# First attention's context normalisation: split between two VectorE passes instead of one ScalarE pass

## The reference, cut to what matters

```
x = x + jnp.tanh(g_xattn[0]) * _L0_xattn_ref(_layernorm(x), ctx_1024, ctx_1024, mask, Wq, bq, Wk, bk, Wv, bv, ln_gamma, ln_beta)
...
scores = jnp.where(mask == 0, -jnp.inf, scores)
probs = jax.nn.softmax(scores, axis=-1)
context = jnp.einsum('bij,bjk->bik', probs, V)
mu = jnp.mean(context, axis=-1, keepdims=True)
var = jnp.var(context, axis=-1, keepdims=True)
normed = (context - mu) * jax.lax.rsqrt(var + EPS)
return normed * ln_gamma + ln_beta
```

## Time and profile before

| | before |
|---|---|
| runs | 553.64, 554.6, 555.0 us; median 554.6 |
| the profiled execution | 555.17 us, its span 553.2 us |
| TensorE's granted clock, mean | 0.933 |
| busy in the span: TensorE, VectorE, ScalarE, GpSimd | 500.8, 394.0, 340.7, 361.3 us |
| the first attention | the start to about 110 us |

### The profile page before, as it was taken

The page is one execution under the profiler, slowest core; times in us unless marked ns, Lnnn a source line. Parts: engine busy times, 40 slices in busy tenths (PEclk is TensorE's granted clock), DMA queues, the critical chain, the costliest instruction groups (busy, mean ns, idle before and its releaser), DMA issues.

```text
span 553.2 us, 12766 instructions
## 1 busy us (share of the span) xinstructions
PE 500.8 (91%) x3611; PEld 332.6 (60%) x3611; DVE 394.0 (71%) x1174; ACT 340.7 (62%) x997; POOL 361.3 (65%) x780
## 2 busy tenths in 40 slices
PE   6888797599999998799999999999999999999952
PEld 5767685456666665565656565666666565656520
DVE  3769788457433443358999898989999999988631
ACT  3667686412255553298777777777777777777510
POOL 3664788877045555324878787878878787877442
PEclk9979897579999999889999999999999999999965
DMA  8855340021122221000000000000000000000000
GB/s 232 154 94 150 92 145 16 24 87 54 29 73 72 81 71 52 27 5 7 15 18 14 21 11 21 11 20 12 21 11 21 11 22 11 19 12 7 11 10 5
DMA packets 32452, 24.48 MB, mean 44 GB/s; under 512 B 7912, under 2 KB 29808, under 8 KB 32352
## 3 DMA queue, kind: packets, MB, share of 16 engines
q1 hardware_dynamic: 29392, 18.17, 13.3%
q0 software_dynamic: 2272, 4.67, 2.6%
q10 hardware_dynamic: 720, 0.82, 0.6%
HBM read 16.88 MB, written 8.39 MB: 46 GB/s over the span
## 4 chain that ended last, share of the span: by engine, by line
PE 70%; POOL 5%; DVE 3%; DMA 3%; issue 3%; ACT 1%; POOLq 0%; SPq 0%; DVEq 0%
PE bank L1309 13%; PE bank L1257 12%; PE bank L1270 8%; PE bank L1248 7%; PE bank L992 5%; PE bank L1008 2%; PE bank L1281 2%; PE bank L1318 2%; PE bank L946 2%; PE bank L947 2%; PE bank L957 2%; DMA xs<-sorted_x 2%; PE bank L1244 2%; PE bank L1297 1%; PE bank L1234 1%
## 5 line engine op out<-in xcount | busy, mean ns | idle before, releaser
L1358 ACT ACTIVATE PRT<-bank 77x512 f32<-77x512 f32 x128 | 74.7, 584 | 18.2 <-PE bank L1257 18.2
L1257 PE MATMUL bank<-cst,wgu 128*77 128x128 f32 x512 | 81.0, 281 | 0.6 <-ACT wgu L1350 0.6
L1309 PE MATMUL bank<-w,xn3T 128*128 128x512 f32 x128 | 74.9, 668 | 2.5 <-DVE XN L1505 2.0
L936 POOL DMA_INDIRECT routed<-ys,to x39 | 37.3, 956 | 46.4 <-DVE ys L1139 37.0
L1350 ACT ACTIVATE wgu<-wgu,low 128x77 f32<-128x77 f32 x256 | 67.3, 346 | 0.4 <-DVE low L1451 0.3
L1257 PEld LDWEIGHTS bank<-cst,wgu 128*77 128x77 f32 x512 | 58.4, 148 | 14.9 <-issue 7.9
L1437 DVE TENSOR_TENSOR wgu<-bank,biasQ 128x616 f32<-128x616 f32 x64 | 50.9, 796 | 9.0 <-PE bank L1248 6.1
L1270 PE MATMUL bank<-PRT,VP 77*32 77x128 f32 x1024 | 54.5, 285 | 0.7 <-ACT PRT L1358 0.7
L1505 DVE TENSOR_TENSOR XN<-bank,OH 128x512 f32<-128x512 f32 x64 | 44.3, 692 | 14.1 <-PE bank L1309 11.3
L1248 PE MATMUL bank<-KB,QT 32*128 32x308 f32 x256 | 51.3, 437 | 0.0
L1444 DVE TENSOR_REDUCE top<-wgu 128x8 f32<-128x616 f32 x64 | 50.5, 789 | 1.1
(11 more groups left out here) (230 smaller groups left out, 1262.3 us busy)
## 6 DMA issues: line engine op xcount, KB each, us to landing
xs<-sorted_x SPq DMA_DIRECT2D x39, 64.5 KB, 1.8
wgu<-in_wgu SPq DMA_DIRECT2D x4, 512.0 KB
y<-routed SPq DMA_DIRECT2D x32, 64.0 KB, 1.8
out<-res SPq DMA_DIRECT2D x32, 64.0 KB, 1.7
ctxT<-in_ctxT SPq DMA_DIRECT2D x16, 77.0 KB, 2.8
mask<-in_mask SPq DMA_DIRECT2D x16, 77.0 KB, 3.5
wdn<-in_wdn SPq DMA_DIRECT2D x2, 512.0 KB
X<-in_x SPq DMA_DIRECT2D x1, 768.0 KB, 5.6
```

Source lines behind the costliest of these rows:

```text
L1257: last = nc.tensor.transpose(bP[c % 2][0:SK, j * 128:j * 128 + 128], SC[u][:, c * HG + j, :], ident)
L1309: nc.tensor.matmul(bF[:, :], xn3T[u][:, :], w2[:, k * HT:(k + 1) * HT, :], start=True, stop=True).then_inc(s["f"], 1)
L1358: nc.scalar.activation(PT[c % 2][:, :], bP[c % 2][0:SK, :], ACT.Copy if c * HG < HH else ACT.Exp).then_inc(s["pTs"], 1)
```

## The change

The normalised context was made by ScalarE as context x inverse deviation + shift, and VectorE multiplied it by gamma and added it to X. Now VectorE makes (context - mean) x gamma from PSUM in one operation per batch (`centred`), and adds that times the inverse deviation to X in one operation per batch (`residual`). ScalarE's `normed` is gone, and so are GpSimd's two operations for the shift. `shifted` moved behind `attend_stats`. GpSimd's `inv_std0` now waits for the residual of the pair two before, where it waited for the normalisation of the pair two before.

```diff
-        def normed(g):
-            act.wait_ge(s["inv"], g + 1)
-            wait(act, s["zg"], g - 1)
-            for b in range(PAIR):
-                last = nc.scalar.activation(z[g % 2][:, b, :], U[g % 2][:, b, 0:D], ACT.Identity, bias=nr[g % 2][:, b:b + 1],
-                                            scale=ru[g % 2][:, b:b + 1])
-            last.then_inc(s["z"], 1)
...
-        written_out(NG, [(unit, 19), (values_1, 3), (norm1, 6), (probs_T, 3), (keys, 0), (normed, 4), (exps, 2), (rows_T, 0), (norm1_T, 6)])
+        written_out(NG, [(unit, 19), (values_1, 3), (norm1, 6), (probs_T, 3), (keys, 0), (exps, 2), (rows_T, 0), (norm1_T, 6)])
...
+        def centred(g):
+            u = g % 2
+            dve.wait_ge(s["umv"], g + 1)
+            wait(dve, s["zg"], g - 1)
+            for b in range(PAIR):
+                last = nc.vector.scalar_tensor_tensor(out=z[u][:, b, :], in0=U[u][:, b, 0:D], scalar=mv[u][:, b, 0:1],
+                                                      in1=gain, op0=ALU.subtract, op1=ALU.mult)
+            last.then_inc(s["z"], 1)
+
         def residual(g):
             u = g % 2
+            dve.wait_ge(s["inv"], g + 1)
+            dve.wait_ge(s["sh"], g + 1)
             dve.wait_ge(s["z"], g + 1)
-            nc.vector.tensor_tensor(z[u][:, :, :], z[u][:, :, :], spread(gain), ALU.mult).then_inc(s["q"], 1)
-            dve.wait_ge(s["sh"], g + 1)
-            dve.wait_ge(s["q"], 5 + g)
             wait(dve, s["inv1"], g - 1)
-            x = X[:, pair(g), :]
-            nc.vector.tensor_tensor(x, x, z[u][:, :, :], ALU.add).then_inc(s["zg"], 1)
+            for b in range(PAIR):
+                x = X[:, PAIR * g + b, :]
+                last = nc.vector.scalar_tensor_tensor(out=x, in0=z[u][:, b, :], scalar=ru[u][:, b:b + 1], in1=x,
+                                                      op0=ALU.mult, op1=ALU.add)
+            last.then_inc(s["zg"], 1)
...
-        written_out(NG, [(route, 10), (values_0, 5), (shifted, 5), (attend_stats, 6), (residual, 7), (masked, 3), (slots, 10), (mask_bias, 0), (unit, 20)])
+        written_out(NG, [(route, 10), (values_0, 5), (attend_stats, 6), (shifted, 5), (centred, 6), (residual, 7), (masked, 3), (slots, 10), (mask_bias, 0), (unit, 20)])
...
             pool.wait_ge(s["umv"], g + 1)
-            wait(pool, s["z"], g - 1)
-            count(nc.gpsimd.tensor_tensor(vr[u][:, :], es[u][:, :], es[u][:, :], ALU.mult))
-            then(nc.gpsimd.tensor_tensor(nm[u][:, :], mv[u][:, :, 0], minus[:, 0:1].to_broadcast([128, PAIR]), ALU.mult))
+            wait(pool, s["zg"], g - 1)
+            then(nc.gpsimd.tensor_tensor(vr[u][:, :], es[u][:, :], es[u][:, :], ALU.mult))
             then(nc.gpsimd.tensor_tensor(vr[u][:, :], vr[u][:, :], mv[u][:, :, 1], ALU.add))
-            then(nc.gpsimd.tensor_tensor(ru[u][:, :], vr[u][:, :], power[:, 0:PAIR], ALU.pow))
-            nc.gpsimd.tensor_tensor(nr[u][:, :], nm[u][:, :], ru[u][:, :], ALU.mult).then_inc(s["inv"], 1)
+            nc.gpsimd.tensor_tensor(ru[u][:, :], vr[u][:, :], power[:, 0:PAIR], ALU.pow).then_inc(s["inv"], 1)
```

More of the change, by code:

```diff
@@ L379, in attend_0 @@
     ru = [sb(f"ru{u}", [128, PAIR]) for u in two]
-    nm = [sb(f"nm{u}", [128, PAIR]) for u in two]
-    nr = [sb(f"nr{u}", [128, PAIR]) for u in two]
     z = [halves(units["sg"][u], 0) for u in two]
```

## The result

The changed kernel took 549.12 us in the median of four runs (547.99 to 549.85), the kernel before 554.8 beside it (553.64 to 556.17): a ratio of 0.9884, interval 0.9841 to 0.9927. Executions of one kernel differ here by 1% and more, so ratios have intervals of 0.2 to 0.5% each way. Shorter distances are read from the profiles, counted from VectorE's second values addition ("V1"), since the loads at the start put V1 anywhere from 18.3 to 20.4 us.

What follows compares the result with a forecast made beforehand. VectorE was taken to set the first attention's pace up to 81 us, GpSimd from 80.90. The walk gave 2.0 us at the last L860 plus 0.1 for clock, 2.1 us: 555.2 to 553.1 profiled, about 552.5 in runs; range 549.8 to 555.0.

Steps and rivals of the forecast that it cites:

- Step (1): Around 25 us: exponentials run at about 21.5 instead of 24.84, and VectorE reaches the statistics about 1.2 us earlier.
- Step (2): From 34.02 us: GpSimd's long inversion, TensorE's XN multiplication and VectorE's L691 at 41.60 all move 2.1 us earlier.
- Step (3): After 41.60 us VectorE sets the pace, losing 0.33 once and 0.2 a turn; L691 at 65.14 comes about 2.3 us earlier.
- Steps (4) to (6): After 65.14 us: 1.2 us left at about 83, 1.8 earlier at 92.47, last L860 2.0 earlier, at about 101.9.
- VectorE's term: Each attention turn: two fused pairs of 0.60 us, next operation after 0.50, cost VectorE 0.2 us more.
- more gain: TensorE's waits before three pairs' values shrink, its clock stays full, VectorE's pairs reach their lower bound: 4.7 us, 550 us; chance 0.17.
- The slower rival: VectorE's residual pair waits for GpSimd's power operation, up to 0.7 us more each turn: 556.5 us; chance 0.10.
- The change does not reach the path: The attention's tail alone sets the end, gaining one turn's 0.4 us: 554.2 us; counted within "same", chance 0.28.
- A sign of being wrong that came: In the attention, VectorE waiting for a mask or another load after 34 us would show the forecast wrong.

Runs made afterwards that it cites:

- The second profile: Changed kernel with three scatters meant to follow the attention, GpSimd's instruction order being unchanged: 549.5 us, ratio 0.9924; its profile repeats the changed kernel's attention.
- the run with all three parts back: Changed kernel with two ScalarE copies, GpSimd's two operations and the early beta addition put back, leaving VectorE's fused arithmetic: 555.4 us, ratio 0.9994.
- the orders alone: Kernel before with exponentials ahead of the normalisation (ratio 0.998), beta addition behind the statistics (0.9982), or both (0.9972).
- the kernel before with the late load: Kernel before with the position table's wide load issued just ahead of the wait that needs it: 555.79 us, ratio 1.0007.

## Why the prediction was wrong

- **Step (1), the exponentials: right.** They ran at 22.41, 2.0 us after V1, before 5.4. The wait for ScalarE at 24.98 is gone.
- **Step (2), as far as XN: about right.** All of the chain to TensorE's XN multiplication was to move 2.1 us; it moved 2.40. The power operation of GpSimd's long inversion began 2.34 us earlier (12.63 us after V1, 14.97 before), and it was shorter. GpSimd's timeline after the change:

```profile
33.03 1.64 POOL L839 TENSOR_TENSOR rstd<-var,power 128x8 f32<-128x8 f32 x1
...
36.71 0.70 POOL L851 TENSOR_TENSOR ru<-vr,power 128x2 f32<-128x2 f32 x1
```

  The power operation for eight batches took 2.02 us before, 0.38 more. I had put 0.15 for collisions with VectorE there. That they are the cause of the 0.38 is not shown (see the last section).
- **Step (2), behind XN: this is where the forecast failed.** It moved L691 by the same 2.1 us, said that VectorE "still waits, 1 us", and gave a fuller clock 0.1 us for the whole phase. From the XN multiplication to VectorE's addition it had been 2.86 us at half clock; it is 1.80 at full clock, and VectorE stands no more. The 1.06 us between the two are the wait that the forecast kept. I took the half clock behind TensorE's wait as given. The second profile, where TensorE still waits 2.67 us there, has the same 1.80.
- **Step (3) inherited it, and charged too much.** The 0.33 us at a wait did not come due, as there was no wait, and 0.2 a turn did not show: at V7 1.4 us were to be left, and 3.52 were (33.12 us after V1 before, 29.60 after). The two turns from V5 to V7 took 10.94 us before and 10.88 after; why VectorE's longer pairs don't show in these two is open. V9 was to come 2.3 us earlier and came 5.28: of the 3.0 missed, 2.1 are there at V7, 0.56 are the clock's at V9 at most, and the chain to XN gave the other 0.3.
- **Steps (4) to (6): sizes right, again without the wait.** From V9 to V15 the forecast lost 0.5 us; measured is a gain of 0.17, the old wait of 1.38 against 0.19 and a little more for each of six turns. GpSimd from L849 to L859, where it does not wait, takes 1.27 us (90.79 to 92.06), 1.28 forecast. Its last turn begins at 98.85, not 101.9:

```profile
90.79 0.21 POOL L849 TENSOR_TENSOR vr<-es 128x2 f32<-128x2 f32 x1
...
92.06 0.18 POOL L859 TENSOR_TENSOR ve<-mv,eps 128x2 f32<-128x2 f32 x1
```

- **VectorE's term: right.** Pairs of 0.60 and the next operation after 0.51 to 0.53 were forecast as 0.60 and 0.50. The estimate from the Trainium skill (VectorE: DVE Perf Modes, the TRN2 errata), 0.1 us a turn, was too low: 0.19 measured. L713's rows gave the better price.
- **The rival that came true is "more gain",** which had 0.17. Its arithmetic (550 us, with 0.8 us at two of the three places that it names; with all three it comes to 549.1) and half of its mechanism fit: the clock is full at all three places, and what lies behind TensorE's XN multiplication got shorter by 1.06, 0.56 and 0.72 us. But TensorE's waits did not shrink, and VectorE's pairs are not at their lower bound. That the sum comes out near the measured time is in part luck: it holds 1 us for those pairs that never came, and nothing for the lead that step (3) charged away. The argument against it was that TensorE would still wait over 2 us in two places. The trace of before already had the row that weakens this: at 54.20 a wait of 2.26 us is followed by multiplications at full clock.
- **The slower rival is refuted by rows.** GpSimd's power operation ran from 36.71 for 0.70 us, and VectorE's residual pair began inside it:

```profile
36.75 0.61 DVE L742 SCALAR_TENSOR_TENSOR X<-sg,ru,X 128x128 f32<-128x128 f32 x2
```

  It took 0.61, as it did beside nothing; all 16 pairs took 0.60 or 0.61. For this pair of operations the trace disagrees with the half of the rule in the Trainium skill (SBUF — State Buffer, Who interferes with whom) that VectorE waits when GpSimd comes first.
- **"The change does not reach the path"** is refuted by the time, 5.7 us in place of 0.4, and by the table: all of the 5.45 us won at V15 reach the last routing.
- **A sign of being wrong that came:** a mask that VectorE waits for after 34 us. It waits 1.38 us at 34.63, and 0.51 at 34.02 before. It cost nothing that step (2) had not given up already.

A remainder stays open: why the turns with half clock begin at just the places where they do. The same instructions with the same wait were followed by it in one execution and not in another, and no rule for it was tested. So a part of V5's 1.06 us can belong to the executions that were profiled. The values ahead of V5 ran at or near half clock (1.79 to 1.91 us) in five of the six profiles of the kernel before, its variants and the run with all three parts back, and in two of the seven profiles of the changed kernel and its other variants.

## What to carry to other kernels

At each wait write down the clock of the work behind it, from the rows: half-clock work behind a wait is part of its price, and a forecast that only shifts the wait in time keeps that price without saying so. Before a pattern of waits and clocks is called the effect of an edit, look at a second profile of the same instructions: here one turn's half clock came and went with nothing changed, and was worth 1.3 us. Check that an edit changes the order of the instructions that reach the engine; the one with the scatters did not. And price an edit with all of its companions: here the orders alone gave nothing, the arithmetic alone gave nothing, and all together won 6 us of the attention.

## What the hardware showed that was not expected

- A wait of TensorE of over 2 us is followed by half clock in some places (2.74 us ahead of 38.74, multiplications of values in 1.91 us) and by full clock in others (2.26 us ahead of 54.20 before, 2.05 us ahead of 86.28 after, 1.03 us). Two executions of the same instructions had 2.49 us ahead of V5, one with 1.91 us behind it and one with 1.03.
- GpSimd's power operation on 128x8 took 2.02 us in two profiles (the kernel before, at 34.39, and the run with all three parts back) and 1.64 or 1.65 in the eleven others. VectorE's additions and products of two SBUF tensors beside it don't explain that by themselves. In the kernel before with the late load it took 1.64 with two of them inside it:

```profile
34.86 1.64 POOL L838 TENSOR_TENSOR rstd<-var,power 128x8 f32<-128x8 f32 x1
```

```profile
35.11 0.39 DVE L738 TENSOR_TENSOR sg<-sg,rows 128x256 f32<-128x256 f32 x1
35.60 0.43 DVE L743 TENSOR_TENSOR X<-X,sg 128x256 f32<-128x256 f32 x1
```

  In the two profiles with 2.02 us, and in no other, such an addition begins 0.11 to 0.12 us behind the power operation's start, as here before the change. No run tested whether that is the cause.

```profile
34.39 2.02 POOL L838 TENSOR_TENSOR rstd<-var,power 128x8 f32<-128x8 f32 x1
```

```profile
34.51 0.41 DVE L705 TENSOR_TENSOR X<-X,rows 128x256 f32<-128x256 f32 x1
```
